# A layer of local attention: GpSimd's gathers for the next rows wait for one of ScalarE's exponentials

## The reference

```python
xn = _layernorm(x, axis=-1)
x = x + _L0_attn_ref(xn, ...) + _L0_ffn_ref(xn, ...)
...
xn = _layernorm(x, axis=-1)
x = x + _L2_attn_ref(xn, ...) + _L2_ffn_ref(xn, ...)   # a state-space branch; a mixture of 8 experts, 2 per token
xn = _layernorm(x, axis=-1)
x = x + _L3_attn_ref(xn, ...) + _L3_ffn_ref(xn, ...)   # the layer of this case
```

```python
base = (j > i) & (j <= i + W)          # W = 128, j over the 256 keys of two blocks
scores = jnp.einsum('bhnqd,bhnkd->bhnqk', qb, k2) * scale
scores = jnp.where(mask[None, None], scores, -1e30)
p = jax.nn.softmax(scores, axis=-1)
out = jnp.einsum('bhnqk,bhnkd->bhnqd', p, v2)
```

## Time and profile before

| what | value |
|---|---|
| runs | 3250.82, 3257.53, 3258.21 us; median 3257.53 |
| the profiled execution, its own time | 3265.37 us |
| its span, first to last instruction | 3263.7 us |
| TensorE's mean granted clock | 0.940 of full speed |
| TensorE busy | 2919.4 us, 89% |
| VectorE busy | 1855.6 us, 57% |
| ScalarE busy | 1379.5 us, 42% |
| GpSimd busy | 327.3 us, 10% |
| gathers issued (L2077), whole kernel | 72 |

### The profile page before, as it was taken

One profiled execution on the slowest core, in us unless ns is written; L12 is line 12 of the kernel. 1 busy time (PEld: TensorE's weight loads), 2 busy tenths in 40 slices (PEclk: granted clock), 3 DMA queues, 4 the chain that ended last, 5 costly groups with the idle time before them and its releaser, 6 DMA issues.

```text
span 3263.7 us, 50711 instructions
## 1 busy us (share of the span) xinstructions
PE 2919.4 (89%) x14374; PEld 1828.7 (56%) x14407; DVE 1855.6 (57%) x4470; ACT 1379.5 (42%) x1993; POOL 327.3 (10%) x353
## 2 busy tenths in 40 slices
PE   5999999999989888888789989999997798888888
PEld 3455545554544444444357767766664466666666
DVE  5656665666547777777646666652223555444442
ACT  1544454445425555554454554433232333333333
POOL 0000000000000000000211121121112211111110
PEclk7999999999878999999999999999998899999999
DMA  6433543254122121212230110132211433333340
GB/s 207 138 103 85 162 138 106 81 162 138 55 72 63 57 66 59 63 61 66 76 139 32 51 45 32 45 112 84 86 61 55 123 82 65 91 91 92 78 89 17
DMA packets 144299, 279.77 MB, mean 86 GB/s; under 512 B 22384, under 2 KB 80113, under 8 KB 134161
## 3 DMA queue, kind: packets, MB, share of 16 engines
q1 hardware_dynamic: 131760, 244.90, 26.1%
q0 software_dynamic: 10464, 28.59, 3.1%
q10 hardware_dynamic: 2016, 5.58, 0.5%
HBM read 179.31 MB, written 99.68 MB: 85 GB/s over the span
## 4 chain that ended last, share of the span: by engine, by line
PE 74%; DVE 9%; issue 5%; ACT 4%; DMA 4%; another core or an unknown queue 1%; SPq 1%; DVEq 0%; POOL 0%; ACTq 0%; POOLq 0%
PE bank_u L559 6%; PE pair L599 5%; PE pair L543 5%; PE pair L700 4%; PE pair L1984 4%; PE bank L2426 3%; PE bank L488 3%; DVE nmax L870 3%; PE pair L2883 3%; PE bank_m L2847 3%; PE pair L744 3%; PE bank L2847 3%; PE bank L520 2%; PE pair L499 2%; PE pair L1406 2%
## 5 line engine op out<-in xcount | busy, mean ns | idle before, releaser
L776 ACT ACTIVATE probs<-pair 128x1024 f32<-128x1024 f32 x512 | 501.2, 1020 | 220.2 <-PE pair L543 219.1
L870 DVE TENSOR_REDUCE nmax<-bank 128x1 f32<-128x512 f32 x664 | 442.2, 686 | 210.6 <-PE bank L520 147.8
L870 DVE TENSOR_REDUCE nmax<-bank_m 128x1 f32<-128x512 f32 x360 | 246.7, 685 | 114.5 <-PE bank_m L520 67.6
L559 PE MATMUL bank_u<-probs,vext 128*32 128x512 f32 x2048 | 294.0, 648 | 0.6 <-ACT uraw L763 0.5
L520 PE MATMUL bank<-k_a,q_a 96*128 96x512 f32 x336 | 173.6, 551 | 24.1 <-DMA k_a<-parts_dram 20.6
L543 PE MATMUL pair<-q_a,k_a 98*128 98x512 f32 x512 | 172.6, 444 | 17.1 <-ACT probs L776 11.8
L2019 ACT ACTIVATE probs<-pair 128x896 f32<-128x896 f32 x128 | 115.8, 918 | 131.1 <-PE pair L1906 78.1
L2116 DVE CUSTOM_DVE_ANT_0 bank<-bank,mask_q 128x128 f32<-128x128 f32 (+1 forms) x320 | 118.6, 416 | 80.1 <-PE bank L1888 73.1
L543 PEld LDWEIGHTS pair<-q_a,k_a 98*128 98x128 f32 x512 | 89.2, 199 | 112.5 <-ACT probs L776 65.3
L1379 PE MATMUL bank<-k,q 62*128 62x512 f32 x302 | 115.2, 485 | 26.7 <-DVE nmax L870 26.7
L1984 PE MATMUL pair<-fc,hid 128*128 128x256 f32 x512 | 131.2, 382 | 6.0 <-ACT probs L2019 6.0
(11 more groups left out here) (422 smaller groups left out, 5946.2 us busy)
## 6 DMA issues: line engine op xcount, KB each, us to landing
parts_dram<-parts SPq DMA_DIRECT2D x64, 512.0 KB, 2.8
q_a<-parts_dram SPq DMA_DIRECT2D x31, 512.0 KB, 5.3
k_a<-parts_dram SPq DMA_DIRECT2D x31, 512.0 KB, 7.2
q<-parts_dram SPq DMA_DIRECT2D x97, 128.0 KB, 2.6
xs<-xres SPq DMA_DIRECT2D x24, 512.0 KB, 3.0
xl<-xs SPq DMA_DIRECT2D x24, 512.0 KB, 3.9
x_in<-xg SPq DMA_DIRECT2D x74, 128.0 KB, 2.1
yg_dram<-y_out POOLq DMA_DIRECT2D x72, 128.0 KB, 2.0
```

The costliest lines, as they stand in the source:

```text
L559: ins = nc.tensor.matmul(bank_u[32 * h:32 * h + 32, :], vext[:, kt, kv(g, h), :], probs[:, kt % 2, h * SEQ:(h + 1) * SEQ], start=(kt == 0) ...
L776: nc.scalar.activation(probs[:, kt % 2, hp * 2 * SEQ:hp * 2 * SEQ + n], st.tile(l, name)[:, 0:n], ACT.Exp).then_inc(st.free["act"].sem, 1)
L870: nc.vector.tensor_reduce(nmax[:, g % 2, qt, h:h + 1], sc.tile(l, name)[:], AX, ALU.max, negate=True).then_inc(sc.free["dve"].sem, 1)
```

## The change

The program of GpSimd for the layer, `pool3`, gets a wait and a fence before `pool_gather_rows`, in steps that have a back half. The wait is for the semaphore value by which ScalarE says that it has finished tile ("E", 2, 0), the exponential of the first head of group 2, in this round. Nothing else is touched.

```diff
--- before.py
+++ after.py
@@ -2203,6 +2203,9 @@
                     fence(pool)
                 pool.wait_ge(*stack_ready(l, it, 2))
                 fence(pool)
+                if BACK[l]:
+                    pool.wait_ge(*done(st, l, it, ("E", 2, 0)))
+                    fence(pool)
                 pool_gather_rows(pool, l, it)
             step.end()
```

## The result

Ten runs of the changed kernel have a median of 3268.04 us (3266.64 to 3271.8), beside 3258.18 (3250.82 to 3265.16, ten runs) for the kernel before on the same chip: ratio 1.0029, 95% interval 1.0018 to 1.0039. It is slower by 9.9 us, just about what a measurement of this kernel can tell from no change, and not the 15.4 us faster that was forecast. The profiled execution took 3267.42 us, its span is 3265.4.

The account below looks back on a forecast made before the run. TensorE, busy 89% of the span, was taken as the bound, idled by a ScalarE stall beside gathers in seven rounds. Gain 3.87 - 1.3 = 2.6 us in six rounds, 15.4 in all: 3265.4 becomes 3250.0 (median 3242), range 3196 to 3266.

Parts of the forecast that it names:

- The size of the stall with its tail: Local-attention loop, fourth round, weighing to output matmuls: stall and tail lose 9.0 us, of which 1.8 is the tail.
- that case: Rival, VectorE lengthens the gathers: its 2.9 us of work added to their length cancels the gain; 3258 us, chance 0.03.
- the price of a handoff beside gathers: TensorE-to-ScalarE handoffs at the new place: each 3.35 us late, as in the first round, capped at the stretch's end, 2887.8.
- (2, 3) late, (3, 0) late, and two shorter waits: Fourth round's turns: (2, 3) done 2877.3, seen 2880.7; (3, 0) seen 2882.1; (3, 1) seen 2887.8; outputs begin 2890.55.
- it only moves: Rival: nothing passes from 3.3 us after the first gather; gain 3.87 - 2.9 per round, 3251; chance 0.20 with another cause.
- the slow clock: TensorE's lowered clock falling partly on output matmuls: 0.42 lost per us, 0.6 to 2.1 us a round, taken 1.3.
- the earlier start of the outputs: Output matmuls of the fourth round begin at 2890.55, 3.87 us earlier than before the change.
- my own case: Stall moved and shortened: 2.6 us net in six rounds, none in the first; own range 3225 to 3250, chance 0.45.
- The stall vanishes: Rival: at the new place handoffs run unhindered as for VectorE; 60.5 us go, 3197 us; chance 0.22.
- Slower: Rival: nothing passes in either direction from first gather (2876.3) until 2887.8; 3.4 us later per round, 3281; chance 0.10.

Follow-up runs that it names:

- the kernel before's second profile: The kernel before, unaltered, run again for its trace on the same chip as the repeated changed kernel; 3264.4 us in the one profiled run.
- The four pairs: Changed kernel with its eight gathers in four pairs, the later ones waiting on ("E", 3, 0), ("E", 3, 3) and ("S", 1, 0); 3208.39 us, ratio 0.9842.

## Why the prediction was wrong

**Right.** That the gathers make the stall and not the stack loads, whose lateness changes nothing while leaving the gathers out gives back 55 us. The size of the stall with its tail, 9.0 us in the fourth round: without gathers the outputs begin 9.5 us earlier there and 8.4 in the mean round (12.53 instead of 22.07 and 20.90). The first exponential 1.9 us behind the table load in all seven rounds, and the first gather 2.2 us behind its start. The end of the stall at the same distance behind the first gather, forecast 11.47 us, seen 11.66. The gathers are no longer than before (9.88 us from first to last): that case is out. Outputs 20.2 us behind the weighing, inside the 19 to 21 named.

**The step that failed** is the price of a handoff beside gathers. I took 3.35 us from the first round, "whatever holds the handoff lets some through", and built on it (2, 3) late, (3, 0) late, and two shorter waits. At the new place the stretch has two parts instead. At first everything passes at full speed: TensorE's signal due 2.3 us behind the first gather starts the exponential at 2878.99 at once. Then none of TensorE's signals passes, from the one due at 4.0 us to 1.8 us behind the last issue, in any of the seven rounds. What is late is one wait of 8.38 us, not each handoff by 3.35. The nine waits of the earlier trace rows are one in each of six rounds, and three (3.93, 2.18 and 1.25) in the first. What I had read there stands in the rows, and it is there again in the kernel before's second profile:

```profile
2610.14 0.92 ACT L2019 ACTIVATE probs<-pair 128x896 f32<-128x896 f32 x1 [3.36 <-remote]
2611.11 0.61 PE L1903 MATMUL pair<-mask_k,ident_bf 128*128 128x512 bf16 x1 [2.84 <-ACT probs L2019]
...
2612.99 1.73 ACT L2019 ACTIVATE probs<-pair 128x896 f32<-128x896 f32 x2 [1.93 <-PE pair L1906]
```

ScalarE waits 3.36 us, works, and waits again, so that the hold comes in two pieces. The row between them shows again which way is held: ScalarE's signal reaches TensorE within 0.1 us, 9.6 us behind the first gather, while a signal of TensorE to VectorE, due at 2608.27, is recorded at 2613.03. But it is the exception of one round in seven, and it didn't come along to the new place; even the first round of the changed kernel has one whole hold, (3, 1) at 15.72. Why that round of the kernel before splits it was not tried. The other six rounds of before spoke for a hold in one piece. I had counted that as a rival, "it only moves", with just this free part of 3.3 us, and gave it (together with another cause) a chance of 0.20. That VectorE is spared, as I took from the earlier trace rows, doesn't hold at the new place either: it waits 9.46 us there.

**The terms that were mis-sized** are the slow clock and the earlier start of the outputs. Forecast were 1.3 us lost in the outputs in my own case and 2.9 for the whole slow stretch in the rival; measured are 2.36 a round. And the outputs begin 1.52 us earlier on average, not 3.87. Two things make that difference. The fourth round on which I built is one of the kernel before's two latest (outputs at 22.07 us behind the table load, mean 20.90), which is 1.17: I took a round for the mean. And behind the hold, which ended 0.3 us later than forecast from the table load, the three exponentials weren't back to back (a wait of 0.98 for a tile that TensorE filled at half clock), so that the outputs began 1.2 us later than forecast. Together: -3.87 + 1.3 was forecast, -1.52 + 2.36 came. The sign turned on these two terms; neither is large.

**The other cases.** "The stall vanishes" (3197) describes what happens when the series is broken or left out, not this change. "Slower" (3281) named the right side and the wrong mechanism: it had everything held from the first gather on, which the exponentials at 2877.73 and 2878.99 refute. The measured 3268.0 lies just above my range, which ended at 3266; "only moves" had the mechanism, and came to 3251 because I let its tail take back 2.9 of a gain of 3.87, where 2.36 of 1.52 came.

## What to carry to other kernels

Gathers issued one behind another from GpSimd can hold TensorE's signals to the other engines, here from some 2 to 5 us behind the first until shortly behind the last. Look for it in the trace (in PRE3 the same series held nothing), and where it is, don't move the series to a better place first: break it. Groups of two to four with a pause between them, each tied to a signal of other work, brought 51 to 54 of the 55 us at the new place and 41 at the old one, where the place alone brought none (between turns) or 32 us (beside the output matmuls). And where a stall is to be moved ahead of a stretch in which TensorE is the bound, count the slow clock behind the gap at full price there.

## What the runs showed of the hardware

- **The hold.** Eight indirect transfers 1.25 us apart hold what TensorE signals to other engines: ScalarE idles 8.38 us, VectorE 9.46 us in the same round, released within 0.08 us. At the old place TensorE's last signal that passes is due 1.7 us behind the first gather and the first held one 3.3 us; at the new place 2.3 and 4.0; beside the outputs 3.6 and 5.3. At the new place ScalarE starts again 1.1, 1.5 and 1.8 us behind the last issue of four, six and eight. TensorE goes on with its queued work, but with gaps (busy 4.03 of 8.40 us). ScalarE's signals to TensorE and the landings of DMAs pass meanwhile; whether VectorE's would was not seen. The Trainium skill, SBUF — State Buffer, section "Who interferes with whom", has it that "PE and ACT never wait on anyone"; that is said of the memory's ports, and these rows show ScalarE waiting beside gathers for a signal. What carries it (the signals' path, the writing of descriptors, the traffic of the landing rows, the profiler's own records) wasn't tried and stays open. The share of the DMA engines alone isn't it: without gathers a stretch at the same place shows 0.99 and no hold, and with the stack loads late the hold is whole at 0.35:

```profile
2853.00:2857.00 4.00, 4.00 (x44) 3.21 (x37) 1.73 (x9) 1.80 (x3) 0.00 (x0) 1.00 0.99 160
2880.80:2889.20 8.40, 3.49 (x37) 2.60 (x30) 0.00 (x0) 0.04 (x2) 5.10 (x6) 0.84 0.35 104
```

- **It differs between chips.** The same kernel takes 3187.7 us on one chip and 3258 to 3261 on others, and on the first, eight gathers beside the exponentials hold nothing (the changed kernel with late loads: (3, 1) at 9.3 us). Why was not found. Each comparison was made on its own chip at one time, so that chip and time can't be told apart. Neither the changed kernel itself nor a broken series was run on the chip without the hold.
- **The best version** of this study with every gather issued is the changed kernel in two series of four: 3204.8 us, ratio 0.9838 to the kernel before. The four pairs (0.9842) can't be told from it.
